# A graph-attention kernel: the gate products of the lagging row block move from the end of the second chunk to the middle of it

## The reference, cut to what matters

```python
h = max(layernorm(x), 0)
Wh = h @ W;  e = leaky_relu(Wh @ a[:F] + (Wh @ a[F:]).T, 0.2)
h_prime = softmax(where(adj > 0, e, -9e15), axis=1) @ Wh
gi = h_prime @ w_ih.T + b_ih;  gh = h @ w_hh.T + b_hh      # 3 x 128 columns each
r = sigmoid(i_r + h_r);  z = sigmoid(i_z + h_z);  n = tanh(i_n + r * h_n)
x = x + (1 - z) * n + z * h
out = x + adj @ (max(layernorm(x), 0) @ W1.T + b1)
```

## Time and profile before

| What | Value |
|---|---|
| median of 3 runs | 1654.03 us (1653.43 to 1655.37) |
| profiled execution, its own time | 1655.58 us |
| its span, first to last instruction | 1653.7 us |
| PE busy | 1541.6 us, 93% |
| DVE busy | 1177.8 us, 71% |
| ACT busy | 1025.4 us, 62% |
| L849, the products of the row blocks | 8192 matmuls, 943.2 us |
| L933, the products of the second phase | 4096 matmuls, 450 us |

### The profile page before, as it was taken

How to read it: one execution, slowest core, us unless ns; L and a number is a source line. 1 busy time by engine, 2 the same in 40 slices (tenths; PEclk the granted TensorE clock), 3 DMA queues, 4 the chain that set the end, 5 groups by cost and what they waited for, 6 DMA issues and landing times.

```text
span 1653.7 us, 35000 instructions
## 1 busy us (share of the span) xinstructions
PE 1541.6 (93%) x13228; PEld 1334.0 (81%) x13260; DVE 1177.8 (71%) x2414; ACT 1025.4 (62%) x1681; POOL 51.7 (3%) x65
## 2 busy tenths in 40 slices
PE   4447999999999999999999999999999999999998
PEld 4335888888888888888888888888888888888887
DVE  7896999999999999999999999999542000000000
ACT  4788999889998999889998999889300000000000
POOL 2120000000000000000000000000000000000000
PEclk9777999999999999999999999999999999999999
DMA  9449889888898888988889889898536444444430
GB/s 336 173 141 365 307 326 336 328 336 322 325 333 332 327 329 332 332 331 324 327 325 340 324 324 338 325 341 324 201 117 236 172 171 171 171 171 171 171 121 14
DMA packets 79747, 446.03 MB, mean 270 GB/s; under 512 B 9120, under 2 KB 38752, under 8 KB 59232
## 3 DMA queue, kind: packets, MB, share of 16 engines
q1 hardware_dynamic: 73664, 440.34, 71.6%
q10 hardware_dynamic: 6048, 5.25, 0.9%
HBM read 361.63 MB, written 83.92 MB: 269 GB/s over the span
## 4 chain that ended last, share of the span: by engine, by line
PE 89%; DVE 4%; issue 2%; DMA 2%; ACT 2%; SPq 0%; DVEq 0%; ACTq 0%
PE A L849 54%; PE A L933 27%; PE GP L872 3%; PE GP L873 2%; PE GQ L891 1%; DVE AE L616 1%; PE GP L874 1%; DMA h_columns<-AE 1%; ACT M L449 1%; DMA M<-in_xb_dram 1%; DVE JK L616 1%; DMA X<-in_adjb_dram 1%; PE TG L880 0%; PE TG L858 0%; PE GP L871 0%
## 5 line engine op out<-in xcount | busy, mean ns | idle before, releaser
L849 PE MATMUL A<-TB,M 128*128 128x259 f16 x8192 | 943.2, 276 | 77.9 <-DVE M L647 40.3
L849 PEld LDWEIGHTS A<-TB,M 128*128 128x128 fp8e4 x8192 | 796.6, 98 | 213.4 <-issue 86.8
L459 ACT ACTIVATE JK<-X 128x4096 uint8<-128x4096 uint32 x124 | 448.0, 3613 | 1.6 <-DMA X<-in_adjb_dram 1.5
L449 ACT ACTIVATE M<-SB,dsteep 128x256 fp8e4<-128x256 f32 x1040 | 429.2, 504 | 0.0
L580 DVE TENSOR_SCALAR Y<-X 128x4096 fp8e4<-128x4096 f32 x128 | 292.8, 2288 | 7.4 <-DMA X<-in_adjb_dram 7.4
L635 DVE TENSOR_SCALAR M<-SB,nd 128x256 fp8e4<-128x256 f32 x1008 | 283.5, 356 | 4.7 <-issue 4.1
L760 DVE SCALAR_TENSOR_TENSOR hp<-A,R 128x256 f32<-128x256 f32 x32 | 13.6, 425 | 373.1 <-PE A L933 371.1
L933 PE MATMUL A<-WG,X 128*128 128x256 f16 x2048 | 225.5, 273 | 0.9 <-DVE WG L717 0.9
L933 PE MATMUL A<-WG,TB 128*128 128x256 f16 x2048 | 224.9, 273 | 0.0
L933 PEld LDWEIGHTS A<-WG,X 128*128 128x128 fp8e4 x2048 | 200.3, 98 | 24.2 <-DVE WG L717 1.1
L933 PEld LDWEIGHTS A<-WG,TB 128*128 128x128 fp8e4 x2048 | 200.4, 98 | 23.2
(11 more groups left out here) (137 smaller groups left out, 714.6 us busy)
## 6 DMA issues: line engine op xcount, KB each, us to landing
X<-in_adjb_dram SPq DMA_DIRECT2D x128, 2048.0 KB, 8.9
mask_bytes<-Y SPq DMA_DIRECT2D x128, 512.0 KB, 3.8
X<-mask_bytes SPq DMA_DIRECT2D x16, 2048.0 KB, 9.1
TB<-mask_bytes SPq DMA_DIRECT2D x16, 2048.0 KB, 9.1
M<-in_xb_dram SPq DMA_DIRECT2D x8, 512.0 KB, 8.6
h_rows<-M SPq DMA_DIRECT2D x8, 512.0 KB, 3.6
R<-in_xb_dram SPq DMA_DIRECT2D x32, 128.0 KB, 7.8
R<-h_rows SPq DMA_DIRECT2D x32, 128.0 KB, 7.5
```

What stands on the lines that cost most here:

```text
L449: ins = nc.scalar.activation(rows(mask1(c), jj), SB[u][:, :], ACT.Sigmoid, scale=STEEP, bias=dsteep[:, j:j + 1], saturate=False)
L459: nc.scalar.activation(to, X[c % 2][:, :].bitcast(u32), ACT.Sign, accum_out=nz[:, bass.ts(g, 1), c:c + 1].rearrange("p g c -> p (g c)")).t ...
L849: ins = nc.tensor.matmul(A[t][m][:, 0:2 * TW + 1], rows((mask1, mask2)[m](c), jj)[:, t * P:(t + 1) * P], TB[:, c * JC + jj, m, 0:2 * TW + ...
```

## The change

The call of gates for block g-1 is taken out of the end of chunk 1 and put between the two halves of chunk 1, behind the 32 products of half 0 and ahead of the 32 of half 1. projected stays at the end of chunk 1. The calls of linears in the second phase keep their order (projected, then gates). No instruction is added or taken away; no other engine's code is touched.

```diff
+                def gates_of(g, u, k):
+                    if in_range(g, 1):
+                        gates(g - 1, 1 - u, k if u else k - 1)
+
                 def linears(g, u, k):
                     if in_range(g, 2):
                         projected(g - 2)
-                    if in_range(g, 1):
-                        gates(g - 1, 1 - u, k if u else k - 1)
+                    gates_of(g, u, k)
 
                 def slot(g, u, k):
                     for c in range(CS):
...
                                 ins.then_inc(c_pe, 1)
                             elif c == CS - 1:
                                 ins.then_inc(e_t0, 1)
+                            elif c == 1:
+                                gates_of(g, u, k)
                         if c == 0:
                             transposes(g)
-                        if c == 1:
-                            linears(g, u, k)
+                        if c == 1 and in_range(g, 2):
+                            projected(g - 2)
```

## The result

| | before | after |
|---|---|---|
| median | 1654.19 us (1653.43 to 1655.37, 5 runs) | 1662.95 us (1661.78 to 1663.38, 5 runs) |
| profiled execution, span | 1655.58, 1653.7 us | 1663.38, 1661.5 us |
| turn: L858 of one row block to the next | 33.79 and 33.90 us | 34.14 us |

The kernel is slower: ratio 1.0051, 95% interval 1.0040 to 1.0061, or 8.8 us. The forecast was 1665.2 us, in a range from 1660.5 to 1671. The turn is the time from one row block to the next.

What follows compares the result with a forecast made beforehand. A ring through PE and ACT was taken to set the 33.78 us turn. Late rz, 12.1 us, less 0.85 in block 1 gave +11.2 us on 1654.03, so 1665.2 us; range 1660.5 to 1671.

Steps and rivals of the forecast that it cites:

- The releaser of PE's stop: Before chunk 0 PE waits for e_ev[0], released by ACT's first two copies of A; 30 stops, 27.3 us in all.
- Gates start at once in mid-chunk: hpT is copied by 727.95, half 0 of chunk 1 ends at 730.94: margin 3.0 us, no added PE wait.
- Gates on PE cost 3.02 us in the new place: Gates between chunk 1's halves take 3.02 us, bounds 2.97 to 3.23; projected alone is left with 0.67 us.
- Rz 0.42 us later: On ACT, L506 waits for the later projected and delays rz by 0.42 us per block, bounds 0.34 to 0.71.
- 28 x 0.42 + 0.30 = 12.1 us: Loss from late rz in blocks 2 to 30: 0.42 us in each of 28, 0.30 in block 30.
- Block 1 gains 0.85 us once: Block 1 has no projected, so rz starts 3.01 us earlier and PE's stop of 0.85 us goes.
- DVE and the masks of chunk 1: L717 and L675 move to about 738.9 and 739.45; chunk 1's mask is released 3.0 us later; nothing late.
- PE's own cost: No-change rival: PE's 0.9 us before chunk 0 is its own, ACT's 0.42 us falls into slack; 1654 us, chance 0.08.
- the ring: Row-block loop through PE and ACT: 18.64 + 0.50 + 14.64 = 33.78 us, the time between PE restarts.
- The faster rival: Gates alone release ACT 3.4 us earlier and PE's stops vanish: 26 us gained, about 1628 us, chance 0.04.
- projected's end would have to move by less than 0.1 us: Condition for a gain, since L506 precedes L511 on ACT; the forecast had projected's end move by three us.
- The clock stayed at 1.00: Against the much-slower rival: longer PE stops lower its clock, 64 us plus the 11, about 1730 us, chance 0.02.

Runs made afterwards that it cites:

- the swapped ACT order: Changed kernel with rz (L511) put ahead of the copy of GQ to GS in ACT's order: 1653.57 us, ratio 0.9996 to the kernel before.
- the fastest kernel: Kernel before with projected and gates in mid-chunk, half 0 of A copied one count earlier, one mask tile per chunk moved from DVE to ACT: 1619.39 us.
- both cuts of the ring: Kernel before with projected and gates between chunk 1's halves: 1637.79 us; or with ACT copying half 0 of A one count earlier: 1638.05 us.

## Why the prediction held, and where its size was off

**The releaser of PE's stop** was inferred from a lag of 0.75 us. It is shown: moving the copies takes the stop away in both kernels, and one more mask tile on ACT in each of the two chunks between rz and the copies makes the turn 0.77 us longer.

**Gates start at once in mid-chunk.** The copy to hpT ends at 730.63 + 0.38 = 731.01 and the first gate product starts at 734.02; no PE wait appears there. The margin was the 3.0 us forecast.

**Gates on PE cost 3.02 us in the new place.** Measured 737.04 - 734.02 = 3.02 us; projected alone takes 741.29 - 740.62 = 0.67 us. The extra boundary costs nothing that the rows can show.

**Rz 0.42 us later.** From PE's restart to rz it was 18.64 us and is 741.89 - 722.84 = 19.05, so rz is 0.41 us later, as forecast. But to the masks of the next block it was 19.14 us and is 742.36 - 722.84 = 19.52. The copy L506 delays L511 by 0.28 us, the lower bound, where 0.31 had been taken, and the masks follow L511 after 0.47 instead of 0.50 us. L506 itself starts 18.77 us behind the restart, where 18.75 was forecast. That makes 0.38, and a turn 0.36 us longer in the blocks inside the loop body (33.79 to 34.15).

**The term that was mis-sized** is "28 x 0.42 + 0.30 = 12.1 us": it measured 8.8 us (the 29 turns took 981.3 us before, 990.1 after). Of the 3.3 us between, 28 x 0.06 = 1.7 us come from the turn being 0.36 and not 0.42 us longer. The rest, 13 x 0.12 = 1.6 us, is one thing that I had not separated: 13 of the turns of before hold the end of ACT's loop body and are longer, 33.90 us. There the masks came 0.60 us behind L511 and not 0.49 (first the loop's end, then inside it), while after the change the distance is 0.48 us at the loop's end too (the last three lines), and 0.47 to 0.48 inside it:

```profile
298.41 0.60 ACT L511 ACTIVATE rz<-GP 128x512 f32<-128x512 f32 x1 [2.54 <-PE GP L874]
299.01 3.31 ACT L449 ACTIVATE M<-SB,dsteep 128x256 fp8e4<-128x256 f32 x8
...
332.32 0.60 ACT L511 ACTIVATE rz<-GP 128x512 f32<-128x512 f32 x1 [2.52 <-PE GP L874]
332.81 3.30 ACT L449 ACTIVATE M<-SB,dsteep 128x256 fp8e4<-128x256 f32 x8
```
```profile
297.72 0.38 ACT L506 ACTIVATE WG<-GQ 128x256 f32 x1 [3.52 <-PE GQ L891]
298.00 0.59 ACT L511 ACTIVATE rz<-GP 128x512 f32<-128x512 f32 x1
298.48 3.29 ACT L449 ACTIVATE M<-SB,dsteep 128x256 fp8e4<-128x256 f32 x8
```

In these turns the loss is only 0.24 us. The three cases fit one reading, which no run tests by itself: at the loop's end the next instruction can't start sooner than about 0.6 us after the instruction that had to wait. One copy, after which the next can start in 0.28 us, is too short to cover that (the swapped ACT order: 0.61), the sigmoid of 0.49 nearly covers it (0.60), both together, 0.76 us, cover it wholly.

The Trainium skill, page "Advanced Engine Details and Errata", section "Control Flow Timing", gives a compare-and-branch as some 108 ns; the 0.11 us at the sigmoid is of that size, the 0.33 us behind the short copy is three times it, and the measurement decides.

**Block 1 gains 0.85 us once.** Its products run through into block 2 without a stop, as forecast: 224 of them stand in one row, where the earlier trace rows has 128 and then a stop.

```profile
151.81 0.38 PE L858 MATMUL TG<-ident,hp 128*128 128x128 f32 x2
158.63 25.22 PE L849 MATMUL A<-TB,M 128*128 128x259 f16 x224
```

The turn of block 1 fell from 33.12 to 32.10 us, so the gain was 1.02 us and not 0.85. The idle time that the profile names (0.85 us) is less than what the stop costs. At 7.16 us for 64 products, block 2 could have started at 162.91 + 14.32 = 177.23 and started at 178.25, 1.02 us later; the row of the last products only ends 0.16 us behind that point. For the same reason the stop of 0.86 us costs 1.0 us in the other blocks: the turn is 33.78 us with it and 32.77 in the fastest kernel, which has none.

The profiled execution after the change is a further 0.70 us ahead at L858 of block 1 (151.81 against 152.51 us). That comes from the first blocks, where TensorE's clock was below full in both and differed: the first chunk of block 1 took 9.81 us at a granted clock of 0.72 before and 9.37 us at 0.75 after. No code there differs, so I don't count it as an effect of the order. Behind the last product lie 0.7 us more in the profiled execution after; what they are is left open. With these, 8.8 - 1.0 - 0.7 + 0.7 = 7.8 us, the difference of the two spans. The turns alone give 8.8 - 1.0 = 7.8 us, to be compared with the forecast of 11.2. The medians lie 8.8 us apart, with an interval from 6.6 to 10.1, so the two measures agree within the noise.

**DVE and the masks of chunk 1.** L717 waits 0.43 us at the copy in the block shown (0.69 us on the mean of 29, once 2.9), and L675 follows at once. Nothing behind them is late, as forecast.

**The rivals.** "PE's own cost" fell with both cuts of the ring. The faster rival was right that the ring could be cut, but not about how: it put the gain at 26 us, and the cuts gave 16 to 18, because DVE was next. With DVE relieved the 29 turns are 31.0 us shorter. Against it the prediction said that projected's end would have to move by less than 0.1 us for a gain. Its own numbers give another limit: L506 started at 735.50 and rz at 738.41, so with 0.31 us between the two projected could end up to 2.6 us later before anything was lost. It moves by 3.02 us, so the direction stood, by 0.4 us. The clock stayed at 1.00 with stops of 1.2 us, and with stops of up to 1.8 us in the kernel before with nine tiles on ACT:

```profile
722.84:756.99 34.15, 32.93 (x281) 28.12 (x281) 33.22 (x67) 30.06 (x50) 0.79 (x1) 1.00 0.87 323
```
```profile
300.00:1000.00 700.00, 665.12 (x5645) 568.86 (x5665) 641.40 (x1251) 642.81 (x1072) 14.79 (x20) 1.00 0.87 321
```

The Trainium skill (page "TensorE: Matmul & The Clock Gate", section "A second HAM failure mode: psum-queue depth-cycling") says that frequent short idles of PE between groups of matmuls make the clock swing. The traces do not bear that out at stops of 1.2 and 1.8 us, one in each row block.

## What to carry to other kernels

When two results are consumed in a fixed order by an engine that stands waiting, what counts is which of them is produced last and how much of the consumer's work then stands behind it: give out first what is consumed first, and let the last product meet the shortest work. Moving only one of the two earlier gains nothing for an engine that is stopped at the other; here moving projected alone changed nothing, moving gates alone cost 9 us, and moving both took 16 us off. Before trusting busy shares, close the ring in time: if the stretches from one engine to the next and back sum to the period, an engine with 3.6 us of idle time per turn can still be the one that sets it, and the same shift of work to it then costs where it would otherwise gain.

## What the runs showed of the hardware

- The end of a loop body on ACT cost 0.11 us behind a waiting instruction whose successor otherwise starts after 0.49 us, 0.33 us where it starts after 0.28 us, and nothing behind 0.76 us of work already released. On DVE 13 stops of 0.3 to 0.4 us ("issue") stand in each of the twelve traces, and with DVE as the bound every second turn is 0.52 us longer (33.72 against 33.20). That these stops are the end of DVE's loop body fits their number and place; that they make up all of the 0.52 us is not shown.
- A boundary between half-precision and float32 matmuls costs nothing that can be read: gates take 3.02 us between products, and gates and projected back to back 3.69 against 3.02 + 0.67 apart.
- With a row block at 32.77 us and PE busy 99.8% of a stretch of 700 us, the granted clock was 1.00.
